# Graph attention on one core: the scores of the single-head layers made source-first, in groups of 3 to 5 destination blocks

## What is computed

```
h = x @ W
s = h @ a_src
d = h @ a_dst
alpha = leaky_relu(s[src] + d[dst], 0.2)
m = segment_max(alpha, dst)
ex = exp(alpha - m[dst])
denom = segment_sum(ex, dst)
w = ex / (denom[dst] + 1e-16)
out = segment_sum(h[src] * w[:, None], dst)
x = gelu(out + b)
```

## Time and profile before

| | us |
|---|---|
| median of 3 runs (lowest, highest) | 3714.07 (3710.34, 3746.61) |
| profiled execution, its own time | 3708.9 |
| its span | 3707.2 |
| heads, first to last score instruction of DVE | 453.1 to 1819.1 |
| single-head layers, first score instruction to the feed-forward's first | 2366.2 to 3517.7 |
| PE, DVE, ACT busy in the span | 3419.1, 2806.4, 2514.1 |

### The profile page before, as it was taken

One profiled execution on the slowest core, in us unless ns is written; L12 is line 12 of the kernel. 1 busy time (PEld: TensorE's weight loads), 2 busy tenths in 40 slices (PEclk: granted clock), 3 DMA queues, 4 the chain that ended last, 5 costly groups with the idle time before them and its releaser, 6 DMA issues. The chain is left out here.

```text
span 3707.2 us, 69969 instructions
## 1 busy us (share of the span) xinstructions
PE 3419.1 (92%) x27369; PEld 2683.0 (72%) x27370; DVE 2806.4 (76%) x4237; ACT 2514.1 (68%) x4068; POOL 317.8 (9%) x280
## 2 busy tenths in 40 slices
PE   6999889999999999999769998799999999999999
PEld 4665566666666666666568998688878888888777
DVE  6999999999999999999762222666655565677594
ACT  4999899999999999999711111466656665676532
POOL 1000011001000010010004444000000000000000
PEclk8999999999999999999859999899999999999999
DMA  4433312122124121121158885422223221433101
GB/s 144 173 109 140 130 57 74 56 63 67 56 69 190 56 74 56 63 66 56 51 180 269 234 242 121 142 105 105 105 86 115 105 105 62 175 115 112 37 15 35
DMA packets 144871, 390.36 MB, mean 105 GB/s; under 512 B 20048, under 2 KB 91550, under 8 KB 126750
## 3 DMA queue, kind: packets, MB, share of 16 engines
q1 hardware_dynamic: 120520, 346.56, 26.7%
q0 software_dynamic: 20816, 36.07, 5.0%
q10 hardware_dynamic: 3206, 3.20, 0.4%
HBM read 327.87 MB, written 61.11 MB: 105 GB/s over the span
## 5 line engine op out<-in xcount | busy, mean ns | idle before, releaser
L923 ACT ACTIVATE hd_probsT<-hd_psT 128x768 f32<-128x768 f32 (+1 forms) x800 | 659.9, 852 | 70.5 <-PE hd_psT L1013 70.5
L1027 PE MATMUL hd_psO<-hd_probsT,hx 128*32 128x128 f32 (+1 forms) x10000 | 571.8, 281 | 129.1 <-ACT hd_probsT L923 129.0
L1546 PE MATMUL ly_psO<-hx_a,ly_probsT 128*128 128x256 f32 x2500 | 584.1, 381 | 0.0
L1027 PEld LDWEIGHTS hd_psO<-hd_probsT,hx 128*32 128x32 f32 (+1 forms) x10000 | 317.3, 108 | 322.5 <-ACT hd_probsT L923 216.0
L1495 ACT ACTIVATE ly_probsT<-ly_psT 128x768 f32<-128x768 f32 (+1 forms) x300 | 248.4, 828 | 392.7 <-PE ly_psT L1535 392.5
L1546 PEld LDWEIGHTS ly_psO<-hx_a,ly_probsT 128*128 128x128 f32 x2500 | 454.1, 190 | 71.4 <-issue 16.6
L1013 PE MATMUL hd_psT<-ident,hd_scores 128*128 128x128 f32 (+1 forms) x3325 | 479.0, 281 | 0.0
L977 DVE SCALAR_TENSOR_TENSOR hd_scores<-el_heads,hx 128x3125 f32<-128x3125 f32 x133 | 460.8, 3465 | 0.0
L981 DVE CUSTOM_DVE_ANT_0 hd_scores<-hd_scores,mask_heads 128x3125 f32<-128x3125 f32 x133 | 453.6, 3411 | 5.7
L914 ACT ACTIVATE hd_scores<-hd_scores,negmax 128x1664 f32<-128x1664 f32 (+1 forms) x266 | 429.9, 1616 | 5.6 <-DVE negmax L981 5.6
L1013 PEld LDWEIGHTS hd_psT<-ident,hd_scores 128*128 128x128 f32 (+1 forms) x3325 | 355.6, 141 | 98.9 <-issue 98.9
(11 more groups left out here) (348 smaller groups left out, 5041.0 us busy)
## 6 DMA issues: line engine op xcount, KB each, us to landing
ly_mask<-mask_dram SPq DMA_DIRECT2D x72, 1568.0 KB, 6.6
moe_w<-in_L_ffn_w SPq DMA_DIRECT2D x144, 512.0 KB, 5.0
mask_heads<-mask_dram SPq DMA_DIRECT2D x46, 1568.0 KB, 6.7
mask_dram<-el_heads SPq DMA_DIRECT2D x196, 196.0 KB, 1.9
el_heads<-el_dram SPq DMA_DIRECT2D x5, 1568.0 KB, 9.7
el_heads<-el_slope_dram SPq DMA_DIRECT2D x5, 1568.0 KB, 13.1
x<-x SPq DMA_DIRECT2D x8, 640.0 KB, 8.4
el_heads<-el_dram POOLq DMA_DIRECT2D x3, 1568.0 KB
```

The source lines that it names most:

```text
L923: nc.scalar.activation(pT[:, gi % 2, 0:w], psT[gi % 2][:, 0:w], ACT.Copy).then_inc(s_ev, 1)
L1027: last = nc.tensor.matmul(psO[B % 3][cg * CH:(cg + 1) * CH, h * P:(h + 1) * P], hx[0:r, tt, c0:c0 + CH], pT[0:r, gi % 2, t * P:(t + 1) * P ...
L1546: last = nc.tensor.matmul(psO[B % 2][:, 0:D], pT[0:r, gi % 2, t * P:(t + 1) * P], hx[B // NB % 2][0:r, tt, 0:D], start=tt == 0, stop=tt == ...
```

## The change

In `layers_phase` the scores are made with the sources on the partitions. A group is 3, 4 or 5 destination blocks (SIZES), six groups in a layer; a step is KC = 2 source tiles for all destinations of the group, 13 steps in a group. In a step DVE makes two SCALAR_TENSOR_TENSORs of 128 x (128 times the size), and one TENSOR_TENSOR adds the mask to both; ACT makes the exponentials in place; PE uses them as they are as stationary operands. The products of a group's blocks go into one PSUM bank each. The tables `hx` get a first column of ones, so that the product has 257 columns and gives the sum of the exponentials too. The score is the smaller of two sums, each of a row over the destinations (u or v, with the maximum taken off) and a number of the source. For that the maximum of a destination has to be known first: since leaky_relu rises, it is that of the largest source score under the mask, so `maxima` is now one custom instruction over `el` and the mask row; `shifts` makes u and v from it, PE and ACT spread them over the partitions (`spread_rows`, `copy_rows`, rows of one or two blocks at a time). Both masks are loaded: the rows as before for `maxima`, and the turned one in pieces for each step, four in flight.

```
-                nc.vector.scalar_tensor_tensor(sc[:, c, :], el[l % 2][:, 0, 0:N], hx[l % 2][:, b, D:D + 1], el[l % 2][:, 1, 0:N],
-                                               ALU.subtract, ALU.min).then_inc(s_lk, 1)
...
+SIZES = (3, 4, 5, 5, 5, 3)
+KC = 2
+RING = 4
...
+            def scores(C):
...
+                if C >= RING:
+                    dve.wait_ge(s_mm, C - RING + 1)
...
+                    last = nc.vector.scalar_tensor_tensor(pb[0:r, s, i, 0:w], rw[0:r, G % 2, 0, 0:w], hx[l % 2][0:r, k, N8:N8 + 1],
+                                                          rw[0:r, G % 2, 1, 0:w], ALU.add, ALU.min)
...
+                nc.vector.tensor_tensor(pb[0:r, s, 0:n, 0:w], pb[0:r, s, 0:n, 0:w], mT[0:r, s, 0:n, 0:w], ALU.add).then_inc(s_msk, 1)
...
+        at_step = {5: (0, 1, 2, 3, 5), 4: (0, 1, 3, 5), 3: (0, 2, 4)}
...
+                masked((G0 + NG) * NCK - 1)
+                if l < LAST:
+                    maxima_part(l + 1, 0)
+                    rows(G0 + NG - 1)
+                    maxima_part(l + 1, 1)
+                    maxima_joined(l + 1)
+                    shifts(G0 + NG)
...
+            def drain(G):
+                act.wait_ge(s_mm, (G + 1) * NCK)
...
+                for d in range(size(G)):
+                    nc.scalar.activation(ob[:, d, :], psO[d][:, 0:D + 1], ACT.Copy).then_inc(s_dr, 1)
...
+                        if k == 0 and G and d < size(G - 1):
+                            pe.wait_ge(s_dr, first_of(G - 1) + d + 1)
+                        m = min(P, w - d * P)
+                        last = nc.tensor.matmul(psO[d][0:m, 0:D + 1], pb[0:r, s, i, d * P:d * P + m], hx[l % 2][0:r, k, 0:D + 1],
+                                                start=k == 0, stop=k == NB - 1)
```

```
-        psO = [ctx.enter_context(nc.psum_tensor(f"hd_psO{i}", [P, 512], F32)) for i in range(3)]
+        psO = [ctx.enter_context(nc.psum_tensor(f"hd_psO{i}", [P, 512], F32)) for i in range(2)]
+        psM = ctx.enter_context(nc.psum_tensor("hd_psM", [P, 512], F32))
...
+                nc.gpsimd.tensor_tensor(rows_, rows_, rden[:, B % 3, :].rearrange("p (h o) -> p h o", o=1).broadcast_to([P, HG, CH]),
+                                        ALU.mult).then_inc(s_y, 1)
...
+            def copy_mask(j):
+                act.wait_ge(s_mT, j + 1)
+                if j >= 2:
+                    act.wait_ge(s_mst[j % 2], stored_upto(j - 2))
...
+                if n % 4 == 1 and n // 4 + 2 < UNITS:
+                    turn_mask(n // 4 + 2)
```

More of the change, by code:

```diff
@@ L1155, in _ @@
             dve.wait_ge(s_first_masks, 32)
+        @block.gpsimd
+        def _(pool):
+            for table in tables:
+                nc.gpsimd.memset(table[:, :, 0:1], 1.0).then_inc(s_one, 1)
+            pool.wait_ge(s_one, len(tables))
         @block.scalar
@@ L1224, in _ @@
                     spread_el(b - 2)
+SIZES = (3, 4, 5, 5, 5, 3)
+NG = len(SIZES)
+STARTS = [sum(SIZES[:i]) for i in range(NG)]
+assert sum(SIZES) == NB
+GW = max(SIZES)
+KC = 2
+NCK = -(-NB // KC)
+RING = 4
+KNOWN = STARTS[NG - 1]
+SPREADS = [-(-n // 2) for n in SIZES]
 @phase
@@ new lines, in rows @@
+            def rows(G):
+                l, n = G // NG, size(G)
+                dve.wait_ge(s_dr, first_of(G) + n)
+                c_(nc.vector.tensor_scalar(rden[:, 0:n], ob[:, 0:n, 0], 1e-16, None, ALU.add))
+                c_.wait()
+                c_(nc.vector.reciprocal(rden[:, 0:n], rden[:, 0:n]))
+                c_.wait()
+                if G == 0:
+                    dve.wait_ge(s_bias, 16 * LAYERS)
+                for d in range(n):
+                    out = ob[:, d, 1:D + 1] if l < LAST else y_last[:, STARTS[G % NG] + d, :]
+                    nc.vector.scalar_tensor_tensor(out, ob[:, d, 1:D + 1], rden[:, d:d + 1], bb[:, l, :],
+                                                   ALU.mult, ALU.add).then_inc(s_y, 1)
@@ L1538, in products @@
-            def products(n):
-                B, gi = n // 4, n % 4
-                pe.wait_ge(s_ev, n + 1)
-                if gi == 0 and B >= 2:
-                    pe.wait_ge(s_y, B - 1)
-                for t in range(TG[gi]):
-                    tt = T0[gi] + t
-                    r = min(P, N - tt * P)
-                    last = nc.tensor.matmul(psO[B % 2][:, 0:D], pT[0:r, gi % 2, t * P:(t + 1) * P], hx[B // NB % 2][0:r, tt, 0:D],
-                                            start=tt == 0, stop=tt == sum(TG) - 1)
-                last.then_inc(s_mm, 1)
+            spread = {"rows": 0, "el": 0}
@@ new lines, in spread_rows @@
+            def spread_rows(G, j):
+                pe.wait_ge(s_uv, G + 1)
+                if spreads_upto(G) + j:
+                    pe.wait_ge(s_row, spreads_upto(G) + j)
+                if spread["el"]:
+                    pe.wait_ge(s_ec, spread["el"])
+                spread["rows"] += 1
+                for d in range(2 * j, min(2 * j + 2, size(G))):
+                    for i in range(2):
+                        o = (d - 2 * j) * 2 * P + i * P
+                        last = nc.tensor.matmul(psR[:, o:o + P], uv[:, G % 2, i, d:d + 1].broadcast_to([P, P]), g["ident"][:, :],
+                                                start=True, stop=True)
+                last.then_inc(s_sp, 1)
```

774 lines of the change are left out of this document (451 added, 323 removed).

## The result

The changed kernel takes 3774.3 us (median of 4; 3769.8 to 3784.6) against 3712.2 (median of 4; 3708.3 to 3746.6): ratio 1.0164, 95% interval 1.0117 to 1.0210. The forecast was 3656, range 3590 to 3730. The profiled execution took 3784.6, 75.7 more than that of before.

| stage, first to last mark | before, us | after, us | forecast |
|---|---|---|---|
| heads, first to last maximum read | 1359.1 | 1368.3 | +9 |
| feed-forward of layer 0 (untouched), first to last hidden product | 360.9 | 373.4 | 0 |
| single-head layers, first DVE instruction to the next phase's first product | 1151.5 | 1202.7 | -72 |

A forecast was written before the change was run, and what follows sets the result against it. DVE was taken to bound the heads, PE the single-head layers. 3708.9 - 67 (layers) + 9 (heads) = 3651 us for the profiled execution, which lay 5 us under the median: 3656, range 3590 to 3730.

The forecast's parts named there:

- the cover at a change of group: Layers: PE enters groups 1 to 3 with three steps ready; wait for the first bank 0.7 us a change.
- rival D: Layers, set up after the measurement: PE's own work is longer whatever it waits for; no chance given.
- rival 4: Layers: 257-column products pipeline worse than 256, 3750 records cost 0.029 us more each, 109 us, total 3765; chance 0.05.
- the granted clock matters little here: Changes of layer: PE's slower clock after a gap counts little, since PE waits for DVE afterwards anyway.
- my 923: PE's work in the layers without bank waits: products 814 us, way into next layer 71, turning back 5, spreading 33.
- The drain: Group changes: PE waits for the first bank's copy, begun after the last product; 0.7 us each, 15 changes, 10 us.
- Where DVE uncovers PE: Layers: maxima in steps 0 to 5 make PE wait, 20.5 us a layer plus 6 in the last, 67 us.
- rival 2: Layers: mask rows are late, heavy steps end with the DMA; 60 to 80 us instead of 9, about 3715; chance 0.16.
- The layers' sum: Layers: 18 + 933 + 67 + 9 + 40 + 12.5 = 1080 us against 1151.5, -72; -67 taken.
- The three signs: Wrong if: heads' block is longer, DVE waits for `ly_mask` over about 3 us a layer, PE waits in a group's second half.
- rival 3: Heads: mask transposes and their copy lengthen the PE-ACT chain past DVE, 112 us, total 3768; chance 0.10.
- the 6 for POOL: Heads: 6 us for `rows` on POOL, which may hold up DVE; bounds 0 and 50 us.

The follow-up runs named there:

- Experiment 6: Changed kernel with 20 transposes of the unit matrix on PE ahead of each group's first product, from group 1 on: 3780.8 us, ratio 1.0196.
- experiment 1: Changed kernel with ACT's drain of the old group after the new group's first exponentials instead of its second: 3767.5 us, ratio 1.0160.
- Experiment 5: Changed kernel with the layers' maxima reading 128 of 3125 columns and starting from -30, mask rows loaded as before: 3698.1 us (one run).
- experiment 9: Changed kernel without the 75 maxima and their 70 mask-row loads, every shift made with one minimum a layer: 3658.0 us, ratio 0.9862.
- experiment 7: Changed kernel with the ring of scores at 5 places instead of 4 and that of the turned mask at 3 instead of 4: 3777.3 us, ratio 1.0183.
- Experiment 12: Changed kernel with one shift a layer, early drain, full last-block weights, and POOL scaling one column a head: 3591.4 us against 3596.2 without the POOL edit.

## Why the prediction was wrong, step by step

Two steps failed. The first is the cover at a change of group: the forecast let PE enter each group with three steps ready and priced the wait for the bank at 0.7 us; in the trace PE had none ready at the start of group 1, and its waits for banks and exponentials are 137.7 us where the sum had 86. The second is PE's own work: the clock behind a wait and the products with 53 columns were put at nothing, and PE's busy time inside the groups was 61 us over the forecast's (so rival D holds in part). Together they are 113 of the 123 us.

**PE's work.** The count and the pace held: 0.217 a record with 257 columns, spreading 0.11 a record; rival 4 is out. Two things were missing. First, the last block's products have 53 columns of weights, and a step of 12 records, four of them with such weights, takes 3.16 instead of 2.60: 0.56 x 12.5 x 3 = 21 us. No row of before showed such a product; I took them to cost the same without saying so. Second, the clock. In layer 0 seven steps that follow a wait are longer than steady ones by 2.1, 1.8, 1.5, 3.1, 2.6, 2.8 and 1.6 us: 15.5. The same reading gives some 12 and 14 in the other layers, 42 in all; there the first step of the last group in layer 1 is at full pace behind the same 1.66 us (3.23 for 4.75). Experiment 6 shows the clock as the cause for groups 4 and 5; for the others I only argue it from the windows. My sentence that "the granted clock matters little here", since PE waits for DVE afterwards anyway, was written for the changes of layer and left it out everywhere else, though the earlier trace rows has the price: 13 transposes in 2.83 us, start to start, for 1.4, behind a wait of 3.28 (I called it a gap of 9). Together 63 us; PE's busy time inside the groups was 984.5 (1011.3 less 26.8 in the frame), 61 over my 923. The two agree better than they should: the 923 held some 13 us of work that stands in the frame, so about 11 us of PE's excess have no name. The Trainium skill has the sum in TensorE: Matmul & The Clock Gate, "HAM oscillation — how this bites in real kernels": a wait between two runs of products makes the second start at the lower clock, and with many waits the starts add up. The trace agrees where the clock fell, with 2.77 us behind a wait of 2.22; behind the 3.26 us of the last layer it had not fallen, and nothing was lost.

**The drain.** "PE waits until the first bank is copied out, which begins only when the last product is through", 0.7 us a change, 10 in all: it was 73.2. I priced the hand-over and not ACT's place in its program: the drain stands behind the exponentials of step 1, and these behind two maxima of DVE. The rows for it were there, since the order of ACT is in the code and the 3.33 us in the earlier trace rows. But the drain's place alone is worth little: with it moved the two waits fall by 12 us of 137.7 (experiment 1). The step that failed beneath it is the lead.

**Where DVE uncovers PE.** The form was right, all maxima in the first half, and 67 + 9 for 64.5 near in size, but by luck: what I gave to heavy steps showed up partly as bank waits. Together 137.7 for 86. I let PE enter each group with three steps ready, in the text for groups 1 to 3; but in group 1 it had none, since the next group's first scores wait for the ring, a place of which is free only as PE ends a step, and its second mask sum for two maxima. DVE's step was also mis-sized: in a group of five it takes 3.00 us (2596.06 to 2599.06) for 2.85, because 3.47 us over 3125 columns is 1.09 ns a column, not 1.04. Experiment 5 gives the price of the maxima, 74 us of the phase, experiment 9 adds 21 in the phase, for their loads and the changes of layer, and 14 ahead of it, and experiment 7 shows that the rows bound the lead too.

**DMA.** Near: 0.59 for 0.6, a mask row in 6.7 us, where the earlier trace rows have 6.6. Waits for mask rows 12.0, 10.3 of them at the start (forecast 4), and nothing like rival 2. The piece of 53 rows never held DVE up: with a ring of only 3 its one wait was 0.18 us. So what the Trainium skill (DMA: Bandwidth & Descriptors, "Why a DMA increments its semaphore by 16 and not by 1") says of such row counts costs nothing here; how long that load runs no row shows.

**Start, changes, end.** 25.7 for 18, mostly the third row's 10.3; 21.8 and 22.0 for 20; 12.5 for 12.5.

**The layers' sum.** +7.7 (start), +4 (changes), +52 (waits), +61 (PE) = 125, against a miss of 123. The three signs that I had named for being wrong were all met: the heads' block is 27.68 us for 27.46, DVE waited 10.3 us for `ly_mask` in layer 0, and PE waited 3.26 us in the second half of a group of the last layer.

**The heads.** +9.2 for +9; rival 3 is out. That the number fits so well is luck, since the 6 for POOL rested on no row. The custom instructions are 8.9 us longer in sum (687.6 for 678.7), nearly the whole. Experiment 12 takes 8 of these back, but the stage gets only 3: a second limit lies 0.03 us a block beneath in the second pass, and the 3 us that I gave to stores stay untested. The Trainium skill (GPSIMD Engine Reference, section 1) names this contention for instructions of DVE with two SBUF inputs; L1024 has two, and the trace agrees.

**Open.** The untouched feed-forward of layer 0 takes 363.8 to 373.4 us in the thirteen profiles of kernels with the new heads and layers, and took 360.9 in that of before. PE waits 16.0 us for gathered rows there against 11.0, and is busy 4 us more. No experiment was made on it; it is 3 to 12 us of the 62 that separate the medians.

## What to carry to other kernels

When an engine becomes free of work, check what it will find ready: count the steps that the engine ahead has finished at the moment of the change, and what stands ahead of each release in its program. A wait of 8.6 us behind one release looked like a matter of order; moved forward, it came back as five waits of 9.8 us in sum, because the work of a third engine behind it was late. Moving a release pays when what it waited behind is early: the same line was worth 12 us beside late maxima and, by subtraction, over 40 without them. And a bound engine that begins to wait can lose twice: look behind each wait for a slow step (here 1.5 to 3 us behind most waits of a group's first products, and nothing behind many others).

## What the runs showed of the hardware

- A product of 257 columns paces as one of 256, 0.433 us for its two records. With 53 columns of weights instead of 128 it is not shorter: a step with two such products in six took 3.16 us for 2.60, 0.28 more for each.
- The granted clock was 0.50 behind a wait of 2.2 us, as behind one of 8.6, and the first step 2.8 us longer in the one case, 1.5 in the other. Behind a wait of 3.26 us in the last layer it was 1.00. 20 transposes that filled the wait of 2.2 us kept the pace; the same 20 ahead of a wait of 6.25 us did not (2.8 us lost).
- DVE's custom instruction with two inputs over 3125 columns takes up to 3.64 us instead of 3.41 beside a multiplication of 128 x 128 on POOL; before, all 199 stood between 3.409 and 3.415.
